# Convolve and rotate on one core: the first sum replaces x in its slot, more of the second pass is loaded before the first ends, and TensorE is given idle matmuls at the start

## The reference, cut to what matters

```python
# x: (16, 128, 64, 64) float32; _gn: normalise each image over groups of 4 channels (mean and variance over 4*64*64)
def _L0_conv_ref(x, weight):        # depthwise 5x5, 16 of the 25 taps are non-zero, made of 8 weights with both signs
    kernel = _build_rpdc_kernel(weight)
    return conv_general_dilated(x, kernel, (1, 1), [(2, 2), (2, 2)], feature_group_count=C)
def _L1_conv_ref(feats, R):         # one 128x128 matrix for each image row h
    return einsum('hvc,bchw->bvhw', R, feats)
x = x + _L0_conv_ref(_gn(x), L0_conv_weight)     # the first sum, x1
x = x + _L1_conv_ref(_gn(x), L1_conv_rota_matrix)
```

## Time and profile before

| what | before |
|---|---|
| median of 3 runs | 454.91 us (453.95 to 457.24) |
| profiled execution, its own time | 454.8 us |
| its span, first to last instruction | 453.0 us |
| PE busy | 401.3 us, 89% |
| DVE, ACT, POOL busy | 363.8, 266.2, 241.7 us |
| DMA | 139.82 MB, mean 309 GB/s |
| mean granted clock of TensorE | 0.962 |

### The profile page before, as it was taken

One profiled execution on the slowest core, in us unless ns is written; L12 is line 12 of the kernel. 1 busy time (PEld: TensorE's weight loads), 2 busy tenths in 40 slices (PEclk: granted clock), 3 DMA queues, 4 the chain that ended last, 5 costly groups with the idle time before them and its releaser, 6 DMA issues.

```text
span 453.0 us, 8510 instructions
## 1 busy us (share of the span) xinstructions
PE 401.3 (89%) x3096; PEld 200.0 (44%) x3096; DVE 363.8 (80%) x691; ACT 266.2 (59%) x516; POOL 241.7 (53%) x312
## 2 busy tenths in 40 slices
PE   0799999999999999799999999999999709999900
PEld 0345555555555555344444444444444304444400
DVE  3699999999999999689989999999868806888800
ACT  2186676675676676656777666666764326677400
POOL 6488675675675676555666655555521123454200
PEclk9999999999999999899999999999999958999975
DMA  8726878799967769769999999999999979999997
GB/s 305 323 59 216 279 220 289 281 362 362 334 221 260 276 202 370 294 260 317 343 320 341 328 325 335 388 297 291 332 328 321 270 114 376 401 417 428 425 427 307
DMA packets 33414, 139.82 MB, mean 309 GB/s; under 512 B 3420, under 2 KB 3548, under 8 KB 20828
## 3 DMA queue, kind: packets, MB, share of 16 engines
q1 hardware_dynamic: 15532, 104.98, 65.7%
q10 hardware_dynamic: 17840, 34.29, 21.5%
HBM read 72.14 MB, written 67.12 MB: 307 GB/s over the span
## 4 chain that ended last, share of the span: by engine, by line
PE 82%; DMA 8%; POOL 2%; DVE 2%; ACT 1%; issue 1%; SPq 0%; ACTq 0%; POOLq 0%
PE ps L695 58%; PE ps L730 22%; DMA x_scratch<-area 4%; DMA norm<-affine 1%; POOL area L407 1%; DMA area<-in_x_dram 1%; DMA area<-x_scratch 1%; PE ps L705 1%; DVE area L611 0%; ACT gn L502 0%; PE ps L713 0%; DVE area L554 0%; DVE stats L565 0%; ACT area L494 0%; POOL gn L430 0%
## 5 line engine op out<-in xcount | busy, mean ns | idle before, releaser
L695 PE MATMUL ps<-area 64*64 64x496 f32 (+2 forms) x2560 | 285.6, 593 | 7.1 <-DVE area L611 4.2
L695 PEld LDWEIGHTS ps<-area 64*64 64x64 f32 x2560 | 141.7, 134 | 104.2 <-issue 92.5
L407 POOL TENSOR_TENSOR area<-mask,area 128x325 f32<-128x325 f32 x128 | 132.5, 1059 | 46.2 <-PE ps L695 32.8
L730 PE MATMUL ps<-gn,rot 128*128 128x512 f32 x256 | 116.3, 607 | 13.2 <-ACT gn L502 13.2
L481 ACT ACTIVATE area<-area,affine 128x256 f32<-128x256 f32 x191 | 97.4, 588 | 33.1 <-DVE affine L584 33.0
L494 ACT ACTIVATE area<-ps 64x512 f32<-64x512 f32 x128 | 75.8, 592 | 28.1 <-PE ps L695 25.4
L565 DVE BATCH_NORM_STATS2 stats<-area 128x6 f32<-128x512 f32 x128 | 80.5, 688 | 4.5 <-DMA area<-in_x_dram 4.5
L730 PEld LDWEIGHTS ps<-gn,rot 128*128 128x128 f32 x256 | 48.0, 193 | 78.6 <-issue 59.4
L574 DVE BATCH_NORM_STATS2 stats<-area 128x6 f32<-128x512 f32 x128 | 81.1, 697 | 1.1
L421 POOL TENSOR_SCALAR area<-area,affine 128x256 f32<-128x256 f32 x62 | 46.1, 753 | 65.3 <-DVE affine L584 65.2
L604 DVE TENSOR_TENSOR tin<-ps,tin 128x512 f32<-128x512 f32 x76 | 51.6, 689 | 16.4 <-PE ps L730 16.4
(11 more groups left out here) (21 smaller groups left out, 68.0 us busy)
## 6 DMA issues: line engine op xcount, KB each, us to landing
x_scratch<-area ACTq DMA_DIRECT2D x64, 512.0 KB, 10.0
area<-in_x_dram SPq DMA_DIRECT2D x31, 1024.0 KB, 6.2
tin<-x_scratch SPq DMA_DIRECT2D x19, 1024.0 KB, 12.4
out_dram<-tin SPq DMA_DIRECT2D x18, 1024.0 KB, 9.8
out_dram<-area SPq DMA_DIRECT2D x13, 1024.0 KB, 27.4
area<-x_scratch SPq DMA_DIRECT2D x7, 1024.0 KB, 18.5
rot<-in_rota_dram SPq DMA_DIRECT2D x4, 1024.0 KB, 9.6
area<-x_scratch SPq DMA_DIRECT2D x2, 896.0 KB, 15.4
```

The costliest lines, as they stand in the source:

```text
L407: last = nc.gpsimd.tensor_tensor(taps[k % TRING][:, c * KW:(c + 1) * KW].rearrange("p d (b r) -> p d b r", r=TAPS), mask[:].rearrange("p d ...
L695: last = nc.tensor.matmul(ps[half, bank + c].rearrange("p (j w) -> p j w", j=J)[:, :, outs], taps[k % TRING][rows, (2 * pair + c) * KW + d ...
L730: nc.tensor.matmul(ps[:, rot_bank(m), :], rot[:, n % UNITS * RH + h], gn[n % NRING][:, h], start=True, stop=True).then_inc(rotated, 1)
```

## The change

- x1 is written over x in its slot; the `y` slots go, and two small buffers `spare` hold what ACT takes out of PSUM. x of steps 1 to 31 is laid out as x1 is (channel, image, column). A slot is free only when the x1 in it is stored and measured, so x of step s + 3 is loaded behind waits for that.
- Four buffers `kept` and the x slots: granules 16 to 19 (FRONT) are loaded with channels 0 to 63 in steps 26 to 29, 20 to 23 (EARLY) with 0 to 79 in steps 29 to 32, the missing channels of each four in one transfer (`load_rest`, rows of 32 KB); 24 and 25 (PARTED) with 0 to 111 after the last convolution. `tin` has four buffers and a granule is loaded one step later.
- The sends of the norms move from SP to ACT. The x1 stores of steps 30 and 31 move from ACT to SP. (The x1 store of step 0 is eight transfers.)
- PE runs four matmuls on zeros before the first average, and three after it; DVE normalises two images of step 0 and ACT six, before three and five. POOL makes the masks in six instructions, before ten. `taps_first` comes on SP's queue. For granule 15 POOL normalises seven images. `affine` is a ring of 20 rounds.

```diff
 XRING = 6
 GRING = 2
-YRING = 3
...
-DVE_J = 3
+DVE_J = 2
+SPARE = 2
+WARM = (4, 3)
...
-DRING = 5
+DRING = 4
...
+FRONT = range(UNITS, UNITS + 4)
+FRONT_STEP = STEPS_ALL - 6
+FRONT_CHANNELS = 64
+EARLY = range(FRONT.stop, FRONT.stop + 4)
+EARLY_STEP = STEPS_ALL - 3
+EARLY_CHANNELS = 80
+PARTED = range(EARLY.stop, EARLY.stop + 2)
+LATE = C - 4 * GC
...
+        def load_rest(queue, granules, slots, channels, landed):
+            first = granules[0] % UNITS * RH
+            rows = slice(first, first + len(granules) * RH)
+            queue.dma_start(slots[channels], x1_dram[1, channels, rows].rearrange("c (g h) j w -> c g (h j w)", h=RH)
+                            ).then_inc(landed, 16)
...
             for s in range(2, STEPS_ALL + 1):
+                k = s + XRING - 3
+                if XRING <= k < STEPS_ALL:
+                    sp.wait_ge(x1_stored[k % XRING], stores_into(k % XRING, k - XRING))
+                    sp.wait_ge(stats_ready, measured(k - XRING + LAG))
+                    load_x(k)
                 sp.wait_ge(x1_ready, 2 * (s - 1))
-                if s + XRING - 2 < STEPS_ALL:
-                    load_x(s + XRING - 2)
...
+                if s - FRONT_STEP in range(len(FRONT)):
+                    await_stores(sp, s - 3)
+                    load_granule(sp, FRONT[s - FRONT_STEP], slice(0, FRONT_CHANNELS))
...
             def evict(k, pair):
...
-                if pair == 0 and k >= YRING:
-                    act.wait_ge(x1_stored[k % YRING], 32 * (k // YRING))
-                    act.wait_ge(stats_ready, measured(k - YRING + LAG))
+                if q >= SPARE:
+                    act.wait_ge(x1_ready, q - SPARE + 1)
...
+            def warm_up(count):
+                for _ in range(count):
+                    nc.tensor.matmul(ps[0:HALF, 6], half_mean[:], nothing, start=True, stop=True)
+
+            pe.wait_ge(nothing_ready, 1)
+            warm_up(WARM[0])
             for half in (low, high):
                 average_mean(0, half)
             for half in (low, high):
                 average_spread(0, half)
+            warm_up(WARM[1])
```

More of the change, by code:

```diff
@@ L99, in conv_rotate_kernel @@
         own = [sb(f"tin{n}", [C, RH, J * W]) for n in range(DRING)]
+        kept = sb("kept", [C, len(FRONT), RH, J * W])
         def granule_on(a):
@@ L105, in conv_rotate_kernel @@
         tin = [own[n % DRING] for n in range(UNITS)]
-        tin += [granule_on(at_x[n]) for n in (2, 3, 4, 5, 0)] + [granule_on(at_y[2])]
+        tin += [kept[:, n] for n in range(len(FRONT))]
+        tin += [granule_on(at_x[n]) for n in (2, 3, 4, 5)]
         tin += [granule_on(at_n[0]), granule_on(at_n[1]), granule_on(at_t), granule_on(at_t + TILE),
-                granule_on(at_x[1]), own[1], granule_on(at_y[0]), granule_on(at_y[1]), own[2], own[3]]
-        near = sb("near", [P, HALF + BAND])
-        near_middle = sb("near_middle", [P, HALF + BAND])
+                granule_on(at_x[0]), granule_on(at_x[1]), own[0], own[1]]
+        front = kept[:].rearrange("c g h x -> c g (h x)")
+        early = piece(at_x[2], (len(EARLY), RH * J * W))
+        near, near_middle = gn[0][:, 0, 0:HALF + BAND], gn[0][:, 1, 0:HALF + BAND]
+        nothing = gn[1][:, 0]
         mask = sb("mask", [P, KW, BAND])
@@ L188, in x_loads, with stores_of @@
             return k // XRING + (0 if k % XRING == 0 else 1)
+        def stores_of(k):
+            return 2 * GC if k == 0 else 2
         def stores_into(slot, last):
-            return 32 * len(range(slot, last + 1, YRING))
+            return 16 * sum(stores_of(k) for k in range(slot, last + 1, XRING))
         SWITCH = 2 * START
@@ new lines, in _ @@
+            load_rest(sp, FRONT, front, slice(FRONT_CHANNELS, LATE), front_landed)
+            sp.wait_ge(out_stored[UNITS - 1 - DRING], 16)
+            load_granule(sp, UNITS - 1, slice(0, C))
+            sp.wait_ge(convolved, 2 * STEPS_ALL)
+            for n in PARTED:
+                load_granule(sp, n, slice(0, LATE))
+            store(sp, STEPS_ALL - 1)
+            await_stores(sp, STEPS_ALL - 1)
+            load_rest(sp, FRONT, front, slice(LATE, C), front_landed)
+            load_rest(sp, EARLY, early, slice(EARLY_CHANNELS, C), early_landed)
@@ L366, in normalise_granule @@
             engine.wait_ge(in_landed[n], landings(n))
+            if n in FRONT:
+                engine.wait_ge(front_landed, 32)
+            if n in EARLY:
+                engine.wait_ge(early_landed, 16)
             if n >= NRING:
```

202 lines of the change are left out of this document (101 added, 101 removed).

## The result

| what | before | after |
|---|---|---|
| median | 454.43 us (453.81 to 457.24, 4 runs) | 464.77 us (461.34 to 466.44, 4 runs) |
| span of the profiled execution | 453.0 us | 462.5 us |
| mean granted clock of TensorE | 0.962 | 0.951 |

The change makes the kernel slower: ratio 1.023, 95% interval [1.018, 1.027]. The forecast was 445.8 us with a range of 438 to 455. The first two stages did what the forecast said; the end lost more than both had brought.

The account below looks back on a forecast made before the run. It took PE to bound the kernel through the first pass, then the last x1 store and the DMA engines to bound the end. Terms: -3.0 - 4.1 + 0 - 2.0 = -9.1 us on 454.9 us, so 445.8 us; range 438 to 455.

Parts of the forecast that it names:

- Start, -3.0 us: First convolution: matmuls on zeros bring PE in at full pace and VectorE normalises two images for three; -3.0 us.
- The bound of +1.3 us: Start: cost if the pace falls between the two groups of matmuls on zeros, the last three then running at half pace.
- First granules, -4.1 us: Where the first granules begin: norms sent earlier on ScalarE's queue remove PE's gap and slow-clock pair; -4.1 us.
- Steps, 0: Steps of the first pass: x1 over x and SP's waits for landed stores cost nothing; 0 us.
- The cover: Steps: slack of granule loads before GpSimd wants them, 0.6 to 2 us, with some 4 us of ScalarE's idle time behind.
- Rival 5: Granule loads in steps 21 to 31 land late, PE stops in each of ten steps: +18 us, 463.8 us; 8%.
- End, -2.0 us: From the store of granule 11 on: bytes left and their rates end the kernel at 447.7 us against 450; -2.0 us.
- three times the rate of 16, 4.4 us: End: 1.57 MB in 48 channels after the last x1 store, taken as 4.4 us between bounds of 3.8 and 13.1 us.
- +4.0 forecast: End: SP's queue of 9.3 MB at 293 GB/s lands the last x1 store at 371.3 us, before at 367.3 us.
- Rival 2: End: both 48-channel transfers go slowly, at 170 GB/s, 9.3 us each: 454.6 us; 15%.
- The sign that the text gave for being wrong: End: a 48-channel transfer of 9 us, one of three signs that would show the forecast wrong.
- The estimate from the ports: End: by the skill page's port table each 48-channel transfer takes 9.6 us, twice over; +9.5 us on the sum.

Follow-up runs that it names:

- (6): Kernel before with only the new start (seven matmuls on zeros, two images on VectorE for three): 450.4 us, ratio 0.993.
- (7): Kernel before with only the norms of steps 14 and 15 sent from ScalarE's queue: 449.3 us, ratio 0.990.
- kernel 11: Kernel before with the new start and the norm sends on ScalarE's queue, its own early parts kept: 446.8 us, ratio 0.982.
- (1): Changed kernel without any early part of granules 16 to 31, loaded whole after the last x1 store: 447.2 us, ratio 0.985.
- (8): Kernel before with the new start and norm sends, without early parts of granules 16 to 21: 446.0 us, ratio 0.982.
- (3): Changed kernel with FRONT's and EARLY's rest as one 64-channel transfer each, both after the last x1 store: 455.6 us, ratio 1.002.
- 2: Kernel before without its six early partial loads, granules 16 to 21 loaded whole after the last x1 store: 451.9 us, ratio 0.997.
- (5): Changed kernel with the x1 stores of steps 30 and 31 back on ScalarE's queue: 462.8 us, ratio 1.016.
- (13): Kernel (8) with granules 22 to 25 each loaded as four transfers of every fourth channel, 32 channels apiece: 447.3 us, ratio 0.985.
- 12: Kernel (8) with granules 22 to 25 each loaded as four transfers of 32 neighbouring channels: 454.3 us, ratio 1.001.
- 4: Changed kernel with each `load_rest` transfer split into four, one per granule, rows of 8 KB: 464.2 us, ratio 1.023.

## Why the prediction was wrong

By its own steps:

- **Start, -3.0 us: right.** The 22 records from 13.40 us at full pace, and the first pair after at 23.13 us, 2.9 us earlier. Alone it is worth 3.1 us (6). The bound of +1.3 us did not come: the three matmuls behind the averages took 2.79 us, the 2.7 us of full pace, so the pace held over the pause at 8 us. The granted clock reads 1.00 in both kernels (before 13.80 to 20.00 us, after 13.4 to 16.2 us), so it is the time of a record, and not that column, that shows the two paces.
- **First granules, -4.1 us: right.** No gap, and in all 6.94 us of lead at 191.71 us. Alone 4.8 us (7), more than forecast by no more than its interval; with (6), 7.9 us, and kernel 11 shows their sum, 7.4 us by the medians, 8.1 by the ratio.
- **Steps, 0: right** to 329 us. Ahead of the loads of x SP waited twelve times for landed x1 stores, 119.9 us in all and 30.5 us at most. The cover was used: from 190 to 331 us GpSimd waited 14.1 us in six places and ScalarE 8.1 us in four for granules, where neither had waited before, but TensorE was busy for all of the 141 us. In the last step the thin cover that the text named gave way once: granule 13 came late,

```profile
337.99 0.60 ACT L539 ACTIVATE gn<-tin,norm 128x256 f32<-128x256 f32 x1 [6.47 <-DMA tin<-x_scratch]
...
340.57 2.44 ACT L531 ACTIVATE area<-ps 64x512 f32<-64x512 f32 x4
```

ScalarE waited 6.47 us and took the last pairs out of PSUM late. The last x1 store was issued at 344.99 us, 3.9 us later than in the earlier trace rows when the lead is counted. Rival 5 had this mechanism in each of ten steps; it came once, and without the early parts the wait is 0.53 us (1).

- **End, -2.0 us: wrong, and this is the step that failed.** The term was "three times the rate of 16, 4.4 us, as the slow thing seems to be the few partitions written". The reason was right, the inference from it not: three times the partitions did not bring three times the rate. FRONT's last 16 landed at 382.9 us and EARLY's 48 channels at 395.1 us, so these 1.57 MB took 12.2 us, 129 GB/s for 360 forecast: 7.8 us more. FRONT's rest, the same size, stood in front of the last x1 store, where the sum had put it at 293 GB/s with all else: store to landing took 11.5 us more than in the earlier trace rows. PARTED has a part in that, with 229 GB/s from 364 to 370 us for the 293 of the sum; how much is its own no run shows. With the 3.9 us of late issue the store landed at +15.3 us for +4.0 forecast, and from there to the last transfer, at about 460 us, it took 84.3 us for 76.4. The two misses, 11.3 and 7.9 us, are the 19.0 us between 445.8 and 464.8, within a few tenths. A smaller slip is that the sum has seven parts of 16 channels behind the last x1 store of the kernel before; six are issued there (x6 in the earlier trace rows), 0.79 MB.

Rival 2 was this case, at 15% and 454.6 us, and sized at less than half: 8.8 us for 19.0. It took 170 GB/s as its slow end; the bounds of the term had named the right one, 120 GB/s, 13.1 us, and the sum for it was never made: 8.7 us more after the store, 7.7 more in front of it (13.1 for 5.4 at 293 GB/s), 462.2 us. The sign that the text gave for being wrong, a transfer of 48 channels of 9 us, came with 12.2. The estimate from the ports, 9.6 us a transfer, was nearer to 12.2 than the 4.4 taken, and still 2.6 us short. It was put aside for a row that need not speak against it: the x1 stores at 391 GB/s are two halves of 64 partitions issued within 0.7 us of each other, which may be in flight together and reach all 128 between them, and they read SBUF where the pieces write it. No run here has such a half alone. Nor does a run show why the rate is 229 GB/s where the loads of 112 channels are due.

The rest of the diff can be told from (1) and (8): with pieces gone, what remains of the change is 447.2 us, where kernel 8 has 446.0. So the loss of the change lies in its early parts, some 17 us, and its gain in the start and the sends. Of the loss, 9.2 us go when FRONT's rest no longer stands in front of the last x1 store and both rests have 64 channels (3). The early parts as such need not lose: those of the kernel before cost nothing that can be told (2, and 11 against 8).

## What to carry to other kernels

When DMA engines are busy at a share near 1 and move half or less of what they do elsewhere, ask which partitions the transfers touch before asking how many bytes or queues there are. At the rates seen here 64 neighbouring partitions take as long for half a granule as 128 for a whole one, 48 took 12.2 us for what 128 do in 3.8 at 415 GB/s (an estimate), and a store on another queue took 32.58 us to land beside such loads (5). If data must come in parts, a part of every fourth partition cost nothing here (13); if that can't be, as with channels that become ready in order, to wait and load the whole may be faster, as here by some 17 us.

And where the bounds of an unknown term are far apart, write out the whole sum at both, each time the term occurs, also where it stands in front of something on the chain. Here the term stood twice, and was costed once.

## What the runs showed of the hardware

- Loads of 32 partitions, every fourth: 426 GB/s. 32 neighbours: 256. The same size, count and rows (12, 13).
- 64 neighbouring partitions, alone: 210 GB/s, flat over 20 us, at a share of 1.00 (3).
- 16 neighbours, rows of 8 KB: 108 GB/s at a share of 1.01 (before, 369 to 374 us).
- 48 neighbours (80 to 127), with the 16 before and after them: 127 GB/s from 376 to 395 us, whether the rows are 32 or 8 KB (after, 4). In rows of 32 KB 16 packets take about 4.0 us, 131 GB/s; of a transfer to 64 partitions they take 2.56 us (3).
- Where the loads of 112 partitions are due: 229 GB/s at a share of 1.03 (after, 364 to 370 us).
- An x1 store on a queue without loads took 32.6 us to land while loads of 48, 112 and 128 partitions ran on the other queue (5); on SP's queue and without them 6.3 to 9.9 us (1).
- Seven matmuls on zeros, 14 records of 592 to 1085 ns, before and behind the first averages: the convolution that follows runs at 0.124 us a record for 0.220 (after; 6), at a granted clock of 1.00 in both.
